# Moving quarter 2's high/low row split from GpSimd to VectorE in a macaron block (routed FFN, linear attention, routed FFN)

## The reference

```
x = x + 0.5 * ffn(layernorm(x))
x = x + attention(layernorm(x))
x = x + 0.5 * ffn(layernorm(x))

def ffn(x):                       # 8 experts, top 2, F = 512
    probs = softmax(x @ gate_w.T)
    topk_probs, topk_idx = top_k(probs, 2)
    hidden = relu(x @ w1[e] + b1[e]);  out = hidden @ w2[e] + b2[e]
    return sum over the two chosen e of topk_probs * out
```

## Time and profile before

| | us |
|---|---|
| median of 3 runs | 776.9 |
| lowest and highest run | 775.98, 777.06 |
| span of the profiled execution | 648.7 |
| PE, DVE, ACT, POOL busy in the span | 366.4, 359.4, 231.0, 327.5 |

### The profile page before, as it was taken

How to read it: one execution, slowest core, us unless ns; L and a number is a source line. 1 busy time by engine, 2 the same in 40 slices (tenths; PEclk the granted TensorE clock), 3 DMA queues, 4 the chain that set the end, 5 groups by cost and what they waited for, 6 DMA issues and landing times.

```text
span 648.7 us, 13914 instructions
## 1 busy us (share of the span) xinstructions
PE 366.4 (56%) x4927; PEld 341.3 (53%) x4928; DVE 359.4 (55%) x1005; ACT 231.0 (36%) x472; POOL 327.5 (50%) x339
## 2 busy tenths in 40 slices
PE   0300001460079998489898504883088898898940
PEld 0200001450069998388886404773078898798930
DVE  6000019788156555278828798673856754455835
ACT  2200001223035665245652135612163455354520
POOL 6200005178877777755450002477325677777770
PEclk9655555555579999889999856898588999898985
DMA  2000186721191322411030000011401111514135
GB/s 81 26 26 26 47 308 192 296 109 42 46 371 57 138 100 84 180 43 40 34 151 2 1 1 0 27 51 50 171 2 38 47 55 56 212 54 183 50 117 199
DMA packets 20257, 60.17 MB, mean 93 GB/s; under 512 B 6010, under 2 KB 7570, under 8 KB 19018
## 3 DMA queue, kind: packets, MB, share of 16 engines
q1 hardware_dynamic: 11131, 40.77, 17.2%
q0 software_dynamic: 9088, 18.89, 8.0%
HBM read 30.76 MB, written 31.51 MB: 96 GB/s over the span
## 4 chain that ended last, share of the span: by engine, by line
PE 31%; DVE 20%; POOL 18%; SPq 12%; DMA 8%; issue 8%; ACT 2%; POOLq 0%; DVEq 0%; ACTq 0%
POOL xs_dram L492 15%; SPq L344 12%; PE yp L680 7%; PE hp L666 5%; PE hp L668 4%; PE hp L667 4%; PE yp L684 3%; DVE st L1086 3%; DMA yg<-y_dram 3%; DMA x<-in_L_attn_x_dram 2%; DVE x L1338 2%; POOL y_dram L523 2%; PE xTp L658 2%; DVE lnw L1106 2%; DVE hl L1249 1%
## 5 line engine op out<-in xcount | busy, mean ns | idle before, releaser
L523 POOL DMA_INDIRECT y_dram<-yall,kept_numbers x156 | 150.0, 962 | 67.8 <-ACT yall L918 37.3
L1249 DVE SCALAR_TENSOR_TENSOR hl<-hp,hh 128x512 f16<-128x512 f32 x156 | 107.7, 690 | 88.8 <-ACT hh L908 87.8
L492 POOL DMA_INDIRECT xs_dram<-xs,rows x128 | 132.7, 1036 | 38.8 <-issue 34.1
L666 PE MATMUL hp<-xT,w_bytes 128*128 128x128 f16 x624 | 125.7, 226 | 40.0 <-DVE xT L1245 34.8
L908 ACT ACTIVATE hh<-hp 128x512 f16<-128x512 f32 x156 | 93.1, 597 | 132.4 <-PE hp L668 132.3
L668 PE MATMUL hp<-xT,w_bytes 128*128 128x128 f16 x624 | 125.1, 225 | 0.0
L667 PE MATMUL hp<-xT,w_bytes 128*128 128x128 f16 x624 | 125.1, 225 | 0.0
L680 PE MATMUL yp<-w_bytes,hh 128*128 x1248 | 97.9, 223 | 2.2 <-ACT yall L918 2.1
L666 PEld LDWEIGHTS hp<-xT,w_bytes 128*128 x624 | 62.7, 101 | 53.8 <-issue 26.8
L680 PEld LDWEIGHTS yp<-w_bytes,hh 128*128 128x128 f16 x1248 | 78.3, 100 | 3.6 <-ACT yall L918 3.4
L658 PE MATMUL xTp<-ident,xsort 128*128 128x128 f16 x312 | 44.4, 225 | 51.0 <-DMA xsort<-xs_dram 51.0
(11 more groups left out here) (244 smaller groups left out, 613.2 us busy)
## 6 DMA issues: line engine op xcount, KB each, us to landing
xs_dram<-xsort SPq DMA_DIRECT2D x3, 2574.0 KB, 17.0
xsort<-xs_dram SPq DMA_DIRECT2D x8, 792.0 KB
wraw<-y_dram SPq DMA_DIRECT2D x3, 1024.0 KB, 4.9
xs_dram<-xs_dram SPq DMA_DIRECT2D x1, 2574.0 KB
y_dram<-yall,kept_numbers POOLq DMA_INDIRECT x156
xsort<-xs_dram SPq DMA_DIRECT2D x4, 528.0 KB, 3.7
x<-in_L_attn_x_dram SPq DMA_DIRECT2D x4, 512.0 KB, 9.5
yall<-in_L_ffn_w_dram SPq DMA_DIRECT2D x1, 2048.0 KB, 20.4
```

The lines of the kernel that those rows point to most:

```text
L492: g.indirect_dma_start(out=xs_dram[q], out_offset=bass.IndirectOffsetOnAxis(ap=rows[:, q, c:c + 1], axis=0), in_=xs[:, b * J + j, :], in_o ...
L523: g.indirect_dma_start(out=y_dram[q], out_offset=bass.IndirectOffsetOnAxis(ap=kept_numbers[:, q, t:t + 1], axis=0), in_=yall[:, t, :], in_ ...
L666: mm(o, wh, hi, start=True, stop=False)
L1249: v.scalar_tensor_tensor(hl[:, p, :], hp[p][:], 0.0, hh[:, p, :], ALU.max, ALU.subtract).then_inc(s_h_lo, 1)
```

## The change

DVE splits quarter 2's rows too. Its two subtractions stand directly behind its two copies of the transposed rows, as they already did for quarter 1, and POOL's two subtractions for quarter 2 are gone.

```
-        SPLIT_BY_DVE = 1
+        SPLIT_BY_DVE = (1, 2)
...
             for b in attentions(0):
                 beta_added(b)
-            split_rows(2)
             scatter(2)
             for b in attentions(1):
                 beta_added(b)
...
                 last.then_inc(s_xnT_sb[1], 1)
-                if q == SPLIT_BY_DVE:
+                if q in SPLIT_BY_DVE:
                     rowsplit(i - 1, b)
                     rowsplit(i, odd)
```

## The result

The changed kernel takes 779.86 us (median of 20 runs), the kernel before 777.12 (20 runs): a ratio of **1.0036, 95% interval 1.0018 to 1.0053**, so 2.7 us more, between 1.4 and 4.1. The forecast was 779.3 with a range of 777.8 to 780.8.

What follows compares the result with a forecast made beforehand. The prediction took DVE's stream up to quarter 2's `rows`, which opens POOL's scatter, as the bound: 3.77 later less a 1.36 hold gives +2.4, so 776.9 + 2.4 = 779.3 us, range 777.8 to 780.8.

Steps and rivals of the forecast that it cites:

- What opens the scatter: Quarter 2's scatter on POOL is released by DVE's `rows` at 412.23, while POOL's splits have 14.2 us of slack.
- The hold of 1.36: POOL's second split held DVE's small operation after the attention's statistics (line 1092) by 1.36 us, which the change gives back.
- Rival B: At DVE's line 1092: the 1.36 relief doesn't come, as POOL wasn't its cause; +3.8, 780.7; 1 in 20.
- The two splits and the wait: DVE before quarter 2's attention statistics: two splits of 1.17, idling about 1.4 between for ACT; +2.4 at `rows`.
- D: The change does nothing, because DVE has room where quarter 2's splits land; chance counted within a 1 in 50.
- the small form of C: At quarter 2's splits: ACT's high part comes earlier, the wait doesn't bind, the clock dip vanishes; +0.1; 1 in 50.
- C: Quarter 2's scatter waited for POOL's split, so moving it to DVE is faster: 3.3 less, 773.6; 1 in 25.
- Passing it on: From quarter 2's `rows` through scatter, quarter 3 and POOL's later work to the end, the 2.4 us is nowhere lost.
- the difference stays: At the additions of beta, the attention branch's 2.30 slack against POOL is unchanged, since both move by 2.4.
- The sum against the profiled execution: Whole kernel: span 648.7 + 2.4 = 651.1; 128.2 outside the instructions stays, so median 776.9 + 2.4 = 779.3.
- One of its signs of failure: The prediction fails if the distance from quarter 2's `rows` to quarter 3's changes by more than a microsecond.
- A: Quarter 3's preparation: PE's clock fall may leave the chain (+1.5, 778.4) or another come (+3.3, 780.2); 1 in 10 each.

Runs made afterwards that it cites:

- experiment 4: Kernel before, but DVE splits quarter 2's first batch and POOL still the second; 649.95 us (one run) against 650.39 for the kernel before.
- Experiment 3: Changed kernel, with ACT writing quarter 2's second high part ahead of its copy; 784.98 us, ratio 0.9991 (0.9962 to 1.002) against the kernel before.

## Why the prediction was right

*What opens the scatter.* Right: POOL waits for `rows`, never for the split.

*The hold of 1.36.* Right, and shown by moving POOL's split (1.35), by cutting it down (1.34) and by shortening the hold (experiment 4). Rival B falls.

*The two splits and the wait.* Predicted: the first nearly free, a gap of about 1.4, a second of 1.17, +2.4 at `rows`. Measured: 1.35, 1.22 and +2.36. Experiment 3 takes the wait out and gets 1.45 back, experiment 4 gives the second split back to POOL and gets everything back. With this D and the small form of C fall too: the splits landed where DVE had no room, and the wait for ACT did bind.

*Passing it on.* Right in sign and about in size on the 650 kind, which is the kind of the profile that the prediction read. There `rows` came at 414.74 (forecast 414.6), the additions of beta at 456.86 (457.3), and from `rows` to the end of the span it is 236.76 against 236.47. A delay of 16.5 costs 16.1. But the prediction took it that "the difference stays" between the attention branch and POOL, and that was wrong: POOL came 0.55 sooner and the attention 0.87 later, which flipped who came first at the additions of beta and cost 1.1, with the 0.55 won in the scatter.

*The sum against the profiled execution.* The number came out, the reason for carrying it over was wrong. I took the 128.2 between span and median for time outside the instructions. That is 1.75 in the changed kernel's run; the first profile was of an execution of the kind in which the kernel takes 650. In the runs that were forecast the path is another. "After that POOL's longest wait to the end of its work is 0.3" is false there: behind quarter 3's `rows` POOL waits for ACT 69.5 in all, 5.7 at the longest. And DVE does not wait for POOL's additions of beta: they end at 505.54 + 4.64 = 510.18 in the changed kernel's first profile, and DVE's multiplication waits for ACT until 534.99:

```profile
505.54 4.64 POOL L530 TENSOR_TENSOR x<-x,brow 128x1024 f32<-128x1024 f32 x2
...
534.99 1.23 DVE L1391 TENSOR_TENSOR yg<-yg,brow 128x1024 f32<-128x1024 f32 x1 [2.96 <-ACT yg L860]
```

That the change costs 2.7 (1.4 to 4.1) there as well fits a delay passed on, but how it is passed through the long waits stays open. What was earned is the +2.36 at `rows`; that the forecast of 779.3 came so near in runs of a kind whose path it had not seen is in part luck. One of its signs of failure even shows there: from quarter 2's `rows` to quarter 3's it is 122.90 in the changed kernel and 116.80 in the copy of the kernel before. But kernels without DVE's splits have 120.89 and 121.58 there, so that sign tells nothing in this kind. In the 650 kind, for which it was written, it is 95.24 against 94.80, within its microsecond.

*Rivals.* C falls: the slower engine was idle, as the trace said. The rule of the Trainium skill (GPSIMD Engine Reference, Engine selection), about 2x slower for two inputs, has the order of the engines right, 2.11 against 1.22 (1.7x), and taken alone it would give the sign of the kernel's time wrongly. The rule of the Trainium skill on the shared interfaces (GPSIMD Engine Reference, Key points) agrees with the traces: the hold of 1.35 goes with POOL's two-input split. A was not seen where it was put: from quarter 3's statistics to its `rows` it is 43.57 in the changed copy and 43.70 before, on the 650 kind. The clock did move on the chain, but in the attention behind quarter 2's `rows`, where it cost the 0.87 above.

## What to carry to other kernels

Moving an elementwise operation from an idle slow engine to a fast one that opens the next stage costs its length plus whatever it waits for, less any hold that it takes away (here 2.25 + 1.45 - 1.35); look first at which of the two the next stage waits for. Where the slow engine's operation does harm by holding a shared path, move it in time before moving it to another engine: one ACT instruction earlier took the whole hold away at `rows`, though no gain in the time could be measured. Compare a profile's span with the time of its own run before building on it; the gap of 128 us here was another kind of execution, and 1.75 lay outside the span. A profile of the other kind shows other paths, so a sum carried from one to the other is a guess, even where it comes out.

## What the runs showed of the hardware

- In these runs VectorE's operation with two SBUF inputs, when it started under a two-input operation of GpSimd, was not done before that one ended: 1.54 and 0.41 instead of 0.18, 3.28 and 5.25 instead of 1.22. In the other direction GpSimd's indirect DMA, when it started under a two-input operation of VectorE, grew from 0.97 to between 1.01 and 2.00 in quarter 2's scatter. The statistics, with one input, took 3.18 to 3.19 with and without GpSimd beside them.
- One product on TensorE (8 matmuls of 128x128) took 1.05 at a granted clock of 1.00 and 1.80 at 0.58. With the 0.55 that GpSimd came sooner, this turned the order in which VectorE and GpSimd met some 40 us later, and cost 1.1.
- The same kernel takes 650 us in some sessions and 777 to 784 in others, the same chip number among both. In the slower ones, during GpSimd's scatter of quarter 2, TensorE, VectorE and ScalarE stand still for 10 to 30 us at a time, and in four profiles one of their waiting operations starts 3.4 to 4.2 us behind the last scatter; a DMA of the scatter (0.97) and the statistics (3.18) take the same in both kinds. What causes it wasn't tried.
